# Residual rows added by the matrix unit inside the state-space stage, and a last stage that is one memory-to-memory copy

## The chip, the cores and the metric

One core of one Trainium2 chip. The metric is the device time of one launch in microseconds (us): 2570.66 us before, the median of 3 runs (2567.91 to 2570.71).

## The reference, cut to what matters

Two layers over 4096 rows (4 sequences of 1024) of 256 columns, float32. The second one is the place of the change:

```python
xn = _layernorm(x)
x = x + _L1_attn_ref(xn, ...) + _L1_ffn_ref(xn, ...)

def _L1_attn_ref(resid, ...):          # state-space layer
    xn = resid * rsqrt(mean(resid * resid) + eps) * norm_w
    skip = xn @ skip_w.T               # 256 -> 512
    x = xn @ in_w.T
    ...                                # causal convolution, silu, delta, B, C, scan over time
    y = (ys + W_D * x) * silu(skip)
    return resid + y @ out_w.T         # 512 -> 256

def _L1_ffn_ref(x, ...):               # 8 experts, the best 2 for each row, weighted sum
    ...
```

So the output is `x + xn` (called x1p in the kernel), plus the state-space rows `y @ out_w.T`, plus the experts' rows.

## The kernel before

Four stages follow each other, each a block that all engines enter and leave together: `layer0`, `mamba`, `experts`, `combine`. Rows are worked on in 8 chunks of T = 512 (NCH = 8, SUB = 4 groups of 128 rows in a chunk).

**layer0** computes the first layer, x1p = x + xn and what the second layer needs, and stores x1p, xn1, the transposed normed rows xrT (512 KB for each chunk) and the router's logits in device memory (L253 stores x1p).

**mamba** (up to about 1822 us) is a software pipeline of 256 steps u = 32 q + n: q is the chunk, n = 0 to 31 a step in it (channel half n // 16, state n % 16). In each step

- ScalarE makes two decays (L1204, `m_da`), two steps ahead, each of 128x512,
- GpSimd multiplies the step's input (L1058, `bx`, 128x1024), three steps ahead, into one of 5 buffers,
- VectorE runs two scans (L1339, `m_hh`), then multiplies by C (L1347, `hc`),
- TensorE, once VectorE's `hc` of step u has come, broadcasts the C row of step u + 1 into the one PSUM bank `cb` (`spread`, L1408), adds `hc` of step u into `y` (L1434, two matmuls), and then does at most one further piece (`pieces`).

`hc` of step u + 1 waits for `cb` of step u + 1. The pieces are the projections of neighbouring chunks; all of them go through one PSUM bank, `rb`, in an order fixed by the list `ahead`: in chunk q, SK0 to SK3 of chunk q + 1 after steps 0, 2, 4, 6 and IN0 to IN3 of chunk q + 2 after steps 24, 26, 28, 30 (both read `xr`), O0 and O1 of chunk q - 1 after steps 8 and 10 (the output product, L1389), BD and DT of chunk q + 1 after steps 14 to 22. A piece waits until its predecessor has been drained from `rb`, which ScalarE does (`take_in`, `take_skip`, `take_out` ...). The last O0 and O1 follow when the 256 steps are over. GpSimd also adds the convolution taps, does the sums of delta, and sends routed rows away by indirect DMA (`spread_rows`, L1067).

All loads and stores go through SyncE's queue, in an order written out by hand. In chunk q it reads:

```python
load_b(8 * q + 2); load_b(8 * q + 3)     # B rows, 1 MB broadcast, each waits for GpSimd
load_rows(SUB * q + 2)                   # waits for an earlier indirect DMA
if q + 2 < NCH: load_xr(q + 2)           # L906, waits for SK3 of chunk q + 1
load_b(8 * q + 4)
if q > 0: store_rows(q - 1, 0); store_rows(q - 1, 1)   # L926, wait for ScalarE's copy of O0, O1
...
```

**experts** computes the experts and adds their rows into `mo` in device memory by indirect DMAs with addition.

**combine** loads x1p and `mo` in 8 chunks of 512 rows (L1797), adds them on VectorE (L1808) and stores the sum to `out` (L1800), all through SyncE's queue.

Of the kernel before, what the change touches and what calls it, by code (L numbers as in the profile page):

```python
# [6 lines left out]
P = 128  # L7
F32 = mybir.dt.float32
# [4 lines left out]
ALU = mybir.AluOpType  # L13
# [5 lines left out]
D = 256  # L19
KD = D // P  # L20
T = 512
NCH = NTOK // T
CPS = SEQ // T
SUB = T // P
# [32 lines left out]
NJ = NTOK // P  # L57
# [676 lines left out]
KE = E_IN // P  # L734
# [14 lines left out]
def mamba(nc, dram):  # L749
# [5 lines left out]
    HALF = KE // 2  # L755
# [23 lines left out]
    with ExitStack() as ctx:  # L779
        def sb(name, shape, dt=F32):  # L780
            return ctx.enter_context(nc.sbuf_tensor("m_" + name, shape, dt))

        def sem(name):
            return ctx.enter_context(nc.semaphore("m_" + name))
# [4 lines left out]
        rb = ctx.enter_context(nc.psum_tensor("m_rb", [P, T], F32))  # L789
# [3 lines left out]
        w_out = sb("w_out", [P, KE, D])  # L793
        vec = sb("vec", [P, NV1])
        A = sb("A", [P, KE * NST])
        ident = sb("ident", [P, P])
        sel = sb("sel", [3 * 2 * NST, NST], BF16)
        xr = sb("xr", [P, KD, T])
        xpad = sb("xpad", [P, KE, PAD + 2 * T])

        spare = sb("spare", [P, 4, KE, T])
        cv, ez, w, lw = spare[:, 1], spare[:, 1], spare[:, 2], spare[:, 3]
        y1 = [[spare[:, 0, 0:HALF], spare[:, 0, HALF:KE]], [sb("y1", [P, HALF, T])[:]] * 2]
# [17 lines left out]
        mo = sb("mo", [P, 2, D])  # L821
# [24 lines left out]
        ext = part([P, NJ, EXT])  # L846
        onesrow = ones[:, 0:NPICK]
        ps_before, ps_total = y[:, 0], y[:, 1]
        vec_in, w_si_in = sem("vec_in"), sem("w_si_in")
        lg_in, s_c0, s_d, s_ex, s_mm, s_out = sem("lg_in"), sem("c0"), sem("d"), sem("ex"), sem("mm"), sem("plan_out")  # L850

# [12 lines left out]
        block = ctx.enter_context(nc.Block())  # L864
# [22 lines left out]
        @block.sync  # L887
        def _(sp):
            sp.dma_start(lg, dram["logits"]).then_inc(lg_in, 16)
            sp.dma_start(vec[:], dram["vec1"]).then_inc(vec_in, 16)  # L890
            sp.dma_start(w_si[:], dram["w_si"]).then_inc(w_si_in, 16)
            sp.dma_start(xr[:], dram["xrT"][0:P]).then_inc(xr_in, 16)
            for tile, src in w_loads:
                sp.dma_start(tile, src).then_inc(w_in, 16)

            def load_rows(j):
                if j >= NJ:
                    return
                if j >= 2:
                    sp.wait_ge(picks_out[j % 2], 16 * TOPK * (j // 2))  # L900
                sp.dma_start(rows[:, j % 2, 0:D], dram["xn1"][j * P:(j + 1) * P, :]).then_inc(rows_in[j % 2], 16)
                sp.dma_start(rows[:, j % 2, D:REC], dram["ext"][:, j, :]).then_inc(rows_in[j % 2], 16)

            def load_xr(p):
                wait_filled(sp, "SK3", p - 1)
                sp.dma_start(xr[:], dram["xrT"][p * P:(p + 1) * P]).then_inc(xr_in, 16)  # L906

            def store_b(p):
                sp.wait_ge(s_row, p + 1)
                sp.dma_start(bT[p], brow[0:NST]).then_inc(b_out, 16)  # L910

            def load_b(G):
                p, j = G // 8, G % 4
                if p >= NCH:
                    return
                if G % 8 == 0:
                    sp.wait_ge(b_out, 16 * (p + 1))
                if G >= 2:
                    sp.wait_ge(s_bx, (G - 1) * NG)
                src = bT[p:p + 1, j * NG:(j + 1) * NG, :].to_broadcast([P, NG, T])  # L920
                sp.dma_start(bb[:, G % 2], src).then_inc(b_in[G % 2], 16)

            def store_rows(p, j):
                wait_drained(sp, f"O{j}", p)
                at = T + p * T + 2 * j * P
                sp.dma_start(dram["mo"][at:at + 2 * P, :].rearrange("(s p) d -> p s d", p=P), mo[:]).then_inc(mo_out, 16)  # L926

            load_xr(1)
            store_b(0)
            sp.wait_ge(s_d, D_STEPS)  # L930
            sp.dma_start(dram["ext"], ext).then_inc(s_out, 16)
            sp.dma_start(dram["tex"], tex).then_inc(s_out, 16)
            sp.wait_ge(s_out, 32)
            load_rows(0)
            load_rows(1)
            load_b(0)
            load_b(1)
            for q in range(NCH):
                load_b(8 * q + 2)
                load_b(8 * q + 3)  # L940
                load_rows(SUB * q + 2)
                if q + 2 < NCH:
                    load_xr(q + 2)
                load_b(8 * q + 4)
                if q > 0:
                    store_rows(q - 1, 0)
                    store_rows(q - 1, 1)
                load_b(8 * q + 5)
                load_rows(SUB * q + 3)
                if q + 1 < NCH:  # L950
                    store_b(q + 1)
                load_b(8 * q + 6)
                load_b(8 * q + 7)
                load_rows(SUB * q + 4)
                load_b(8 * q + 8)
                load_b(8 * q + 9)
                load_rows(SUB * q + 5)
            store_rows(NCH - 1, 0)
            store_rows(NCH - 1, 1)
            sp.wait_ge(mo_out, 32 * NCH)  # L960
# [395 lines left out]
        def _(pe):  # L1356
            mm = pe.matmul
# [6 lines left out]
            def piece(g, p):  # L1364
                if turn[g, p] > 0:
                    pe.wait_ge(drained, turn[g, p])
                if g[:2] in ("IN", "SK"):
                    e = int(g[2:])
                    if g == "IN0":
                        pe.wait_ge(xr_in, p * 16 + 16)  # L1370
                    col = (E_IN if g[:2] == "IN" else 0) + e * P
                    for k in range(KD):
                        last = mm(rb[:], w_si[:, k, col:col + P], xr[:, k], start=(k == 0), stop=(k == KD - 1))
                elif g == "BD":
                    if p == 0:
                        pe.wait_ge(w_in, 16 * len(w_loads))
                    pe.wait_ge(s_silu, 2 * p + 1)
                    for e in range(KE):
                        last = mm(rb[0:DR + 2 * NST, :], w_x[:, e], xs[p % 2][:, e], start=(e == 0), stop=(e == KE - 1))
                elif g[:2] == "DT":  # L1380
                    e = int(g[2:])
                    wait_drained(pe, "BD", p)
                    last = mm(rb[:], w_dt[:, e * P:(e + 1) * P], dr, start=True, stop=True)
                else:
                    j = int(g[1:])
                    pe.wait_ge(s_y1, 2 * p + 2)
                    for s in (2 * j, 2 * j + 1):
                        for e in range(KE):
                            last = mm(rb[:, (s % 2) * D:(s % 2 + 1) * D], y1[e // HALF][p % 2][:, e % HALF, s * P:(s + 1) * P], w_out[:, e],  # L1389
                                      start=(e == 0 and s % 2 == 0), stop=(e == KE - 1 and s % 2 == 1), skip_group_check=True)  # L1390
                last.then_inc(filled, 1)

            def pieces(q, n):
# [26 lines left out]
            for u in range(STEPS):  # L1420
                q, n = u // NU, u % NU
# [4 lines left out]
                if n % NST == 0:  # L1426
# [3 lines left out]
                    for i in range(HALF):  # L1430
                        e = HALF * j + i
# [346 lines left out]
def combine(nc, dram, out):  # L1778

    with ExitStack() as ctx:  # L1780
        def sb(name, shape, dt=F32):
            return ctx.enter_context(nc.sbuf_tensor("c_" + name, shape, dt))

        def sem(name):
            return ctx.enter_context(nc.semaphore("c_" + name))

        xa = sb("xa", [P, NJ, D])
        mo = sb("mo", [P, NJ, D])
        x_in = [sem(f"x_in{i}") for i in range(NCH)]
        s_add, out_done = sem("add"), sem("out_done")  # L1790
        block = ctx.enter_context(nc.Block())

        @block.sync
        def _(sp):
            for c in range(NCH):
                for tile, src in ((xa, dram["x1p"]), (mo, dram["mo"][T:, :])):
                    sp.dma_start(tile[:, c * SUB:(c + 1) * SUB], src[c * T:(c + 1) * T, :].rearrange("(s p) d -> p s d", p=P)).then_inc(x_in[c], 16)  # L1797
            for c in range(NCH):
                sp.wait_ge(s_add, c + 1)
                sp.dma_start(out[c * T:(c + 1) * T, :].rearrange("(s p) d -> p s d", p=P), xa[:, c * SUB:(c + 1) * SUB]).then_inc(out_done, 16)  # L1800
            sp.wait_ge(out_done, 16 * NCH)

        @block.vector
        def _(dve):
            for c in range(NCH):
                cs = slice(c * SUB, (c + 1) * SUB)
                dve.wait_ge(x_in[c], 32)
                dve.tensor_tensor(xa[:, cs], xa[:, cs], mo[:, cs], ALU.add).then_inc(s_add, 1)  # L1808

# [67 lines left out]
```

## Time and profile before

| | us |
|---|---|
| median of 3 runs | 2570.66 (2567.91 to 2570.71) |
| profiled execution, its own time | 2571.51 |
| its span in the trace | 2569.8 |
| mean granted TensorE clock | 0.95 of full speed |
| TensorE matmul busy | 2128.3 (83%) |
| VectorE busy | 1967.2 (77%) |
| ScalarE busy | 1371.7 (53%) |
| GpSimd busy | 1330.0 (52%) |
| DMA moved | 290.84 MB, mean 113 GB/s |

### The profile page before, as it was taken

What the parts mean: (1) busy time and instruction counts of PE and PEld (TensorE: products, weight loads), DVE (VectorE), ACT (ScalarE), POOL (GpSimd) and SP (SyncE); (2) the same over time, 40 slices, a digit from 0 to 9 for tenths busy, and PEclk for the clock granted to TensorE, in tenths of its full rate; (3) what the DMA queues carried; (4) which work ended last, traced back from release to release, by engine and by line L of the source; (5) the groups of instructions that cost most, each with busy time, mean ns of one, the idle gap of its engine ahead of it and who ended that gap; (6) DMA issues with size and microseconds to landing.
All of it is one profiled execution on the core that took longest, in us unless ns stands there. A gap on an engine that the chain in (4) does not pass through costs nothing. (4 is left out here: it accounts for less than half of the span.)

```text
span 2569.8 us, 34895 instructions
## 1 busy us (share of the span) xinstructions
PE 2128.3 (83%) x10642; PEld 1527.3 (59%) x10642; DVE 1967.2 (77%) x2692; ACT 1371.7 (53%) x2333; POOL 1330.0 (52%) x953
## 2 busy tenths in 40 slices
PE   2699999999976788788888888766599999999991
PEld 1578777787742233333333333332499999999991
DVE  6654566444536999989999999999498888888882
ACT  1322233322346766666666666743377777677760
POOL 1102222022224999999999999996024333433331
PEclk8899999999987999999999999999799999999996
DMA  8010011100121213131313131321466666666746
GB/s 263 17 42 16 25 41 41 41 25 16 41 74 59 103 62 113 66 109 74 113 60 116 61 112 62 105 82 66 173 226 220 208 230 233 217 210 227 236 138 206
DMA packets 117336, 290.84 MB, mean 113 GB/s; under 512 B 20788, under 2 KB 93892, under 8 KB 98452
## 3 DMA queue, kind: packets, MB, share of 16 engines
q1 hardware_dynamic: 102964, 271.31, 30.0%
q0 software_dynamic: 14304, 18.75, 3.6%
q8 instruction: 26, 0.43, 0.1%
q14 instruction: 42, 0.34, 0.0%
HBM read 239.21 MB, written 50.82 MB: 113 GB/s over the span
## 5 line engine op out<-in xcount | busy, mean ns | idle before, releaser
L1058 POOL TENSOR_TENSOR m_work<-m_ux,m_bb 128x1024 f32<-128x1024 f32 x256 | 601.7, 2370 | 37.3 <-DVE m_ux L1317 18.8
L1434 PE MATMUL m_y<-m_work,m_ident 128*128 128x512 f32 x1024 | 498.2, 609 | 1.5 <-DVE m_work L1347 1.5
L1204 ACT ACTIVATE m_da<-m_dl,m_A 128x512 f32<-128x512 f32 x512 | 347.9, 685 | 278.3 <-DVE m_hh L1339 277.5
L1748 PE MATMUL e_h<-e_xTh,e_w1h 128*128 128x256 f32 x1248 | 353.3, 283 | 17.1 <-DVE e_xTl L1684 17.1
L1748 PE MATMUL e_h<-e_xTl,e_w1h 128*128 128x256 f32 x1248 | 349.4, 280 | 0.0
L1748 PE MATMUL e_h<-e_xTh,e_w1l 128*128 128x256 f32 x1248 | 349.2, 280 | 0.0
L1347 DVE TENSOR_TENSOR m_work<-m_hh,m_cb 128x1024 f32<-128x1024 f32 x256 | 312.7, 1222 | 37.7 <-PE m_cb L1408 13.7
L1339 DVE TENSOR_TENSOR_SCAN m_hh<-m_da,m_carry,m_work 128x512 f32<-128x512 f32 x256 | 313.8, 1267 | 11.5 <-POOL m_work L1058 11.5
L1339 DVE TENSOR_TENSOR_SCAN m_hh<-m_da,m_work 128x512 f32<-128x512 f32 x256 | 298.4, 1207 | 14.7 <-POOL m_work L1058 14.5
L1434 PEld LDWEIGHTS m_y<-m_work,m_ident 128*128 128x128 f32 x1024 | 198.8, 194 | 161.8 <-issue 149.8
L281 POOL TENSOR_TENSOR small<-mv,eps_ln 128x4 f32<-128x4 f32 x17 | 3.4, 199 | 551.8 <-DVE mv L399 551.8
L1408 PE MATMUL m_cb<-m_bc,m_sel 96*128 96x512 bf16 x256 | 98.2, 384 | 197.5 <-DVE m_work L1347 197.1
L1748 PEld LDWEIGHTS e_h<-e_xTh,e_w1h 128*128 128x128 f32 x1248 | 237.4, 190 | 17.7 <-DVE e_xTl L1684 17.3
L1647 ACT ACTIVATE e_sg<-e_h,e_b 128x256 f32<-128x256 f32 x312 | 145.8, 467 | 188.5 <-PE e_h L1748 188.5
L1677 DVE TENSOR_TENSOR e_w1l<-e_w,e_w1h 128x1024 fp32r<-128x1024 f32 x156 | 190.8, 1223 | 69.6 <-ACT e_w1h L1628 69.6
L1408 PEld LDWEIGHTS m_cb<-m_bc,m_sel 96*128 96x128 bf16 x256 | 24.7, 97 | 363.6 <-DVE m_work L1347 349.0
L1748 PEld LDWEIGHTS e_h<-e_xTl,e_w1h 128*128 128x128 f32 x1248 | 235.6, 189 | 0.0
L1748 PEld LDWEIGHTS e_h<-e_xTh,e_w1l 128*128 128x128 f32 x1248 | 235.4, 189 | 0.0
L1701 DVE SCALAR_TENSOR_TENSOR e_ac<-e_h,e_b,e_sg 128x256 f32<-128x256 f32 x312 | 149.2, 479 | 44.8 <-ACT e_sg L1647 44.2
L1759 PE MATMUL e_o<-e_w2h,e_ach 128*128 128x256 f32 x624 | 174.1, 279 | 0.0
L1534 POOL DMA_INDIRECT scratch_mo<-e_yo,e_place x78 | 160.8, 2061 | 24.4 <-issue 11.9
L1759 PE MATMUL e_o<-e_w2h,e_acl 128*128 128x256 f32 x624 | 173.3, 278 | 0.0
(263 smaller groups left out, 4755.9 us busy)
## 6 DMA issues: line engine op xcount, KB each, us to landing
e_w<-in_w SPq DMA_DIRECT2D x39, 2048.0 KB, 7.5
m_bb<-scratch_bT SPq DMA_DIRECT2D x64, 1024.0 KB, 4.6
e_w<-in_w SPq DMA_DIRECT2D x39, 1024.0 KB, 10.0
scratch_rec<-x1p SPq DMA_DIRECT2D x39, 260.0 KB, 8.1
e_xg<-scratch_rec SPq DMA_DIRECT2D x39, 260.0 KB, 2.7
e_b<-in_b SPq DMA_DIRECT2D x39, 128.0 KB, 3.0
xt<-in_x SPq DMA_DIRECT2D x9, 512.0 KB, 5.4
xres<-in_x SPq DMA_DIRECT2D x8, 512.0 KB, 4.8
```

Source lines behind the costliest of these rows:

```text
L1058: pool.tensor_tensor(bx[:, u % NB], ux[q % 2][:, cols], slot.to_broadcast([P, HALF, T]), ALU.mult).then_inc(s_bx, 1)
L1204: act.activation(da[d % NA][:], dl[q % 2][:, e], ACT.Exp, scale=A[:, at:at + 1]).then_inc(s_exp, 1)
L1339: dve.tensor_tensor_scan(hh[:, u % 2, i], da[d % NA][:], bx[:, u % NB, i], 0.0 if q % 2 == 0 else carry[:, n % NST, e:e + 1], ALU.mult, AL ...
L1347: dve.tensor_tensor(hc[:, u % 4], hh[:, u % 2], cb[:].rearrange("p (o t) -> p o t", o=1).to_broadcast([P, HALF, T]), ALU.mult).then_inc(s_ ...
L1408: mm(cb[:], sel[:, at:at + 1].to_broadcast([3 * 2 * NST, P]), bc3[q % 2][:], start=True, stop=True).then_inc(s_cb, 1)
L1434: last = mm(y[:, i], ident[:], hc[:, u % 4, i], start=False, stop=(n % NST == NST - 1))
L1534: pool.indirect_dma_start(dram["mo"][:, :], bass.IndirectOffsetOnAxis(ap=place[i][:, s:s + 1], axis=0), yo[i][:, s, :], None, compute_op=A ...
L1647: act.activation(sg[:, m % 2], hbank[m % HR][:, 1], ACT.Silu, bias=b1[i][:, KF + m:KF + m + 1]).then_inc(s_sg, 1)
L1677: dve.tensor_tensor(piece(w1l[i], mm), piece(w1[i], mm), f32(piece(w1h[i], mm)), ALU.subtract).then_inc(s_wl, 1)
L1701: dve.scalar_tensor_tensor(out=ac[:, m % 2], in0=hbank[m % HR][:, 0], scalar=b1[i][:, m:m + 1], in1=sg[:, m % 2], op0=ALU.add, op1=ALU.mul ...
L1748: last = mm(hbank[m % HR][:, j], w[i][:, k, cols], x[i][:, k], start=(p == 0 and k == 0 and j == 0), stop=(p == 2 and k == KD - 1 and j == 1),
L1759: last = mm(obank[i][:, s], a[i][:, m, s * P:(s + 1) * P], w[i][:, m], start=(m + s + p == 0), stop=(p == 2 and m == KF - 1 and s == NS - ...
```

## The change

In mamba, the residual rows x1p of chunk p are loaded into the place of `xr` (`xres` is the same memory, seen as 4 groups of 128 rows by 256 columns), and each O piece begins with two more matmuls, identity times residual rows, that open the accumulation in `rb`. So `mo` holds residual plus state-space rows before the experts add to it. As `xr` and `xres` share their memory, SyncE's order is changed: the residual's load stands where `load_xr` stood, and `load_xr` now follows the stores of O0 and O1. In combine, VectorE's additions and the SBUF tiles go; one DMA copies `mo` to `out`.

```diff
+        xres = xr[:].rearrange("p k t -> p (k t)").rearrange("p (s d) -> p s d", d=D)
...
+            def load_res(p):
+
+                if p + 2 < NCH:
+                    wait_filled(sp, "SK3", p + 2)
+                if p > 0:
+                    wait_filled(sp, "O1", p - 1)
+                sp.dma_start(xres, dram["x1p"][p * T:(p + 1) * T, :].rearrange("(s p) d -> p s d", p=P)).then_inc(res_in, 16)
...
                 load_rows(SUB * q + 2)
-                if q + 2 < NCH:
-                    load_xr(q + 2)
+                if q > 0:
+                    load_res(q - 1)
                 load_b(8 * q + 4)
                 if q > 0:
                     store_rows(q - 1, 0)
                     store_rows(q - 1, 1)
+                if q + 2 < NCH:
+                    if q > 0:
+                        wait_filled(sp, "O1", q - 1)
+                    load_xr(q + 2)
...
+            load_res(NCH - 1)
             store_rows(NCH - 1, 0)
             store_rows(NCH - 1, 1)
...
                     pe.wait_ge(s_y1, 2 * p + 2)
+                    pe.wait_ge(res_in, 16 * (p + 1))
                     for s in (2 * j, 2 * j + 1):
+                        at = slice((s % 2) * D, (s % 2 + 1) * D)
+                        mm(rb[:, at], ident[:], xres[:, s], start=(s % 2 == 0), stop=False, skip_group_check=True)
                         for e in range(KE):
-                            last = mm(rb[:, (s % 2) * D:(s % 2 + 1) * D], y1[e // HALF][p % 2][:, e % HALF, s * P:(s + 1) * P], w_out[:, e],
-                                      start=(e == 0 and s % 2 == 0), stop=(e == KE - 1 and s % 2 == 1), skip_group_check=True)
+                            last = mm(rb[:, at], y1[e // HALF][p % 2][:, e % HALF, s * P:(s + 1) * P], w_out[:, e],
+                                      start=False, stop=(e == KE - 1 and s % 2 == 1), skip_group_check=True)
...
 def combine(nc, dram, out):
...
-            for c in range(NCH):
-                for tile, src in ((xa, dram["x1p"]), (mo, dram["mo"][T:, :])):
-                    sp.dma_start(tile[:, c * SUB:(c + 1) * SUB], src[c * T:(c + 1) * T, :].rearrange("(s p) d -> p s d", p=P)).then_inc(x_in[c], 16)
-            for c in range(NCH):
-                sp.wait_ge(s_add, c + 1)
-                sp.dma_start(out[c * T:(c + 1) * T, :].rearrange("(s p) d -> p s d", p=P), xa[:, c * SUB:(c + 1) * SUB]).then_inc(out_done, 16)
-            sp.wait_ge(out_done, 16 * NCH)
+            sp.dma_start(out.rearrange("(p n) d -> p (n d)", p=P),
+                         dram["mo"][T:, :].rearrange("(p n) d -> p (n d)", p=P)).then_inc(out_done, 16)
+            sp.wait_ge(out_done, 16)
...
-                dve.tensor_tensor(xa[:, cs], xa[:, cs], mo[:, cs], ALU.add).then_inc(s_add, 1)
```

## Rows read from the trace of the kernel before

**Rows 1.** The page's 40 slices: busy tenths, granted clock, DMA.

```profile
DVE  6654566444536999989999999999498888888882
...
POOL 1102222022224999999999999996024333433331
PEclk8899999999987999999999999999799999999996
```

**Rows 2.** Issues of SyncE's queue: start us, us, engine line op out<-in.

```profile
1226.66 0.43 SPq L902 DMA_DIRECT2D m_rows<-scratch_ext  x1
1227.14 0.43 SPq L906 DMA_DIRECT2D m_xr<-scratch_xrT  x1
```

**Rows 3.** Timeline of TensorE around O0 and O1, chunk q = 3.

```profile
1225.26 1.88 PE L1434 MATMUL m_y<-m_work,m_ident 128*128 128x512 f32 x4
1226.97 1.03 PE L1389 MATMUL m_rb<-m_w_out,m_spare 128*128 128x256 f32 x4
1227.84 1.03 PE L1389 MATMUL m_rb<-m_w_out,m_y 128*128 128x256 f32 x4
...
1230.43 0.38 PE L1408 MATMUL m_cb<-m_bc,m_sel 96*128 96x512 bf16 x1
...
1237.79 0.38 PE L1408 MATMUL m_cb<-m_bc,m_sel 96*128 96x512 bf16 x1
```

**Rows 4.** Timeline of VectorE in the same steps; idle time and releaser in brackets.

```profile
1231.04 1.22 DVE L1347 TENSOR_TENSOR m_work<-m_hh,m_cb 128x1024 f32<-128x1024 f32 x1
1232.97 2.46 DVE L1339 TENSOR_TENSOR_SCAN m_hh<-m_da,m_carry,m_work 128x512 f32<-128x512 f32 x2 [0.71 <-POOL m_work L1058]
...
1239.20 1.22 DVE L1347 TENSOR_TENSOR m_work<-m_hh,m_cb 128x1024 f32<-128x1024 f32 x1
```

**Rows 5.** VectorE's waits after step 10 of chunk q = 2.

```profile
1107.60 2.34 DVE L1339 TENSOR_TENSOR_SCAN m_hh<-m_da,m_work 128x512 f32<-128x512 f32 x2 [0.97 <-POOL m_work L1058]
...
1119.44 2.34 DVE L1339 TENSOR_TENSOR_SCAN m_hh<-m_da,m_work 128x512 f32<-128x512 f32 x2 [0.73 <-POOL m_work L1058]
```

**Rows 6.** Time to landing of `load_xr` (L906), and of layer0's loads of 1 KB rows.

```profile
DMA to landing us min/median/max: 3.2/3.4/3.9
...
DMA to landing us min/median/max: 3.4/4.8/6.0
```

**Rows 7.** TensorE's matmuls behind idle times of 3.00 and 3.75 us.

```profile
1216.78 0.58 PE L1408 MATMUL m_cb<-m_bc,m_sel 96*128 96x512 bf16 x1 [3.00 <-DVE m_work L1347]
1217.16 3.14 PE L1434 MATMUL m_y<-m_work,m_ident 128*128 128x512 f32 x4
1220.13 1.88 PE L1373 MATMUL m_rb<-m_xr,m_w_si 128*128 128x512 f32 x4
...
1091.29 0.58 PE L1408 MATMUL m_cb<-m_bc,m_sel 96*128 96x512 bf16 x1 [3.75 <-DVE m_work L1347]
1091.67 3.62 PE L1434 MATMUL m_y<-m_work,m_ident 128*128 128x512 f32 x4
1095.09 2.74 PE L1373 MATMUL m_rb<-m_xr,m_w_si 128*128 128x512 f32 x4
```

**Rows 8.** Stretches: PE, PEld, DVE, ACT, POOL busy us, granted clock, DMA share, GB/s.

```profile
1091.00:1095.00 4.00, 3.71 (x5) 1.65 (x6) 3.61 (x4) 3.58 (x8) 3.92 (x3) 0.50 0.57 231
```

**Rows 9.** Waits of GpSimd in chunk q = 3 (1187.5 to 1313): total, times, longest.

```profile
POOL m_spare L1038 <- ACT m_spare L1182: 2.5, 1, 2.5
POOL m_spare L1032 <- ACT m_spare L1192: 2.1, 1, 2.1
```

**Rows 10.** The end of mamba, on TensorE.

```profile
1812.44 1.10 PE L1389 MATMUL m_rb<-m_w_out,m_spare 128*128 128x256 f32 x4 [1.41 <-DVE m_y L1325]
```

**Rows 11.** Stretches of combine, columns as in the eighth group.

```profile
2539.00:2542.00 3.00, 0.00 (x0) 0.00 (x0) 1.20 (x1) 0.00 (x0) 0.00 (x0) 0.50 1.10 349
...
2563.00:2566.00 3.00, 0.00 (x0) 0.00 (x0) 0.00 (x0) 0.00 (x0) 0.00 (x0) 0.50 1.09 385
```

**Rows 12.** All transfers of combine, window 2531 to 2570.

```profile
DMA packets 12672, 12.58 MB, mean 323 GB/s; under 512 B 384, under 2 KB 12672, under 8 KB 12672
```

More of the change, by code:

```diff
@@ L848, in mamba @@
         ps_before, ps_total = y[:, 0], y[:, 1]
+        res_in = sem("res_in")
         vec_in, w_si_in = sem("vec_in"), sem("w_si_in")
@@ L1780, in combine @@
     with ExitStack() as ctx:
[L1781 to L1790, printed above, removed]
+        out_done = ctx.enter_context(nc.semaphore("c_out_done"))
         block = ctx.enter_context(nc.Block())
@@ L1794, in _ @@
         def _(sp):
-            for c in range(NCH):
-                for tile, src in ((xa, dram["x1p"]), (mo, dram["mo"][T:, :])):
-                    sp.dma_start(tile[:, c * SUB:(c + 1) * SUB], src[c * T:(c + 1) * T, :].rearrange("(s p) d -> p s d", p=P)).then_inc(x_in[c], 16)
-            for c in range(NCH):
-                sp.wait_ge(s_add, c + 1)
-                sp.dma_start(out[c * T:(c + 1) * T, :].rearrange("(s p) d -> p s d", p=P), xa[:, c * SUB:(c + 1) * SUB]).then_inc(out_done, 16)
-            sp.wait_ge(out_done, 16 * NCH)
[L1803 to L1807, printed above, removed]
-                dve.tensor_tensor(xa[:, cs], xa[:, cs], mo[:, cs], ALU.add).then_inc(s_add, 1)
+            sp.dma_start(out.rearrange("(p n) d -> p (n d)", p=P),
+                         dram["mo"][T:, :].rearrange("(p n) d -> p (n d)", p=P)).then_inc(out_done, 16)
+            sp.wait_ge(out_done, 16)
 def kernel(**inputs):
```

## The prediction

> **What bounds the kernel now.** I read the page's slices first [rows 1]. In the state-space stage VectorE and GpSimd are both at 9 tenths and the granted clock is close to full; so what matters there is what delays VectorE. Combine, the last stage, has little VectorE work and much DMA work. The stage before it, the experts, is not touched. Two places therefore decide: combine, which is a plain transfer, and the steps around O0 and O1, where the change puts a wait and matmuls into TensorE's stream.
>
> Next the timelines of one chunk, q = 3, on three engines. TensorE starts O0 at 1226.97, straight behind the sum of step 8, and has the C row for step 10 in `cb` at 1230.43 + 0.38 = 1230.81 [rows 3]. VectorE starts `hc` of step 10 at 1231.04 [rows 4]. So TensorE is only 0.23 us ahead of VectorE there: whatever delays O0 by more delays VectorE. SyncE issues `load_xr` in that chunk at 1227.14, right behind the rows, whose issue hangs on an indirect DMA of GpSimd [rows 2]. That is the place that the residual's load gets. The load is thus issued in the very microsecond in which TensorE wants to begin O0. I looked at the other five chunks in which SyncE's queue stands so (q = 1, 2, 4, 5, 6): the two times are within 0.9 us of each other in all.
>
> Then what VectorE can get back. It waits for GpSimd 0.71 us after step 10 in this chunk [rows 4], 0.97 and 0.73 us in chunk 2 [rows 5]. GpSimd itself works without idle time from late in one chunk far into the next, then waits 2.1 and 2.5 us for ScalarE [rows 9], which follows VectorE's pace. A chunk's chain so runs over GpSimd in its first part and over VectorE in its second.
>
> **The change part by part.**
>
> *The wait for the residual, six chunks (q = 1 to 6).* `load_res` is issued when `load_xr` was, at 1227.14; its own wait, for SK3, was there before, and O1 of the chunk before is long over. Landing takes 3.2 to 3.9 us for `load_xr`, of the same 512 KB; layer0's loads with rows of 1 KB, as this one has, took 3.4 to 6.0, median 4.8, beside other traffic [rows 6]. I take 3.5, near the one in the same place. So TensorE, ready at 1226.97, begins at 1227.14 + 3.5 = 1230.6: 3.6 us late (bounds 3.4 and 5.0).
>
> *The clock.* TensorE now idles 3.6 us there. The nearest rows are idle times of 3.00 and 3.75 us [rows 7]. Behind the first, `cb` took 0.58 for 0.38 and the four records of `y` 3.14 for 1.88: 1.5 us more. Behind the second, 0.2 + 1.74 and then 2.74 for 1.88: 2.8 us more, and the granted clock was 0.50, the 1.2 GHz level, in the stretch behind it [rows 8]. For 3.6 us I take 2.3 (bounds 0 and 3).
>
> *The matmuls.* Two more a piece are four records of 128x256; four of these take 0.87 us from start to start [rows 3]. That is 0.87 for O0.
>
> Together O0 ends 3.6 + 2.3 + 0.9 = 6.8 us later. Less the 0.23 that TensorE was ahead, VectorE's `hc` of step 10 starts 6.5 us later. ScalarE's copy of O0, its store, and O1 follow. SyncE's `load_b` behind the load does not come later, as it waits for GpSimd anyway. Given back: VectorE's next waits for GpSimd, which works on during the stall, 0.7 or 0.97 + 0.73, mean 1.2. Lost again: O1 is 0.9 longer. `cb` of step 12 was done at 1238.17 [rows 3] and VectorE needed it at 1239.20, or 1238.5 without its 0.71 wait [rows 4]; so 0.6 is missing. A chunk costs 6.5 - 1.2 + 0.6 = 5.9 us, six cost 35.
>
> *Chunk q = 7.* Its load has no SK3 to wait for other than past ones, and the queue issues it early, so only the matmuls count: about 0.9 - 0.23 at O0 and the same at O1, 1.3 us.
>
> *The end of mamba.* O0 and O1 of the last chunk stand alone behind VectorE's last product [rows 10], with nothing beside them. The load of their residual lies many steps ahead. 2 x 0.87 = 1.7 us.
>
> *`load_xr` later.* It moves behind the stores of O0 and O1, to about step 12; IN0, which reads it, comes after step 24, over ten steps of about 3.7 us. The load is covered, and would cost its 3.4 us if it were not. `load_b` behind it was issued later than those stores before too. The 4 MB more of DMA traffic find the queue far from full. All this is 0.
>
> *combine.* The stage went from 2531.0 to the span's end, 38.8 us, for 12.58 MB [rows 12] at 349 GB/s while loads and stores mixed, 385 for stores alone [rows 11]. That is 8.39 / 349 + 4.19 / 385 = 34.9, as the first stores overlap the last loads about 36; some 2.8 us are start and end. VectorE's additions, 1.2 us each, lay beside the loads. The copy moves 4.19 MB. No row shows a copy from memory to memory. If an engine moves it as fast as a load or a store, it takes 4.19 / 385 = 10.9 us; if reading and writing share the rate, 8.39 / 385 = 21.8; one after the other, 12.0 + 10.9 = 22.9. The memory's side of the traffic, 8.39 MB, is to be moved either way, so I take 21.8. With 2.4 for start and end the stage is 24.2 us, 14.6 less than before (bounds 25.5 and 13.5).
>
> The Trainium skill, "DMA: Bandwidth & Descriptors", section "Latency and other measured facts", gives 207 to 214 GB/s per direction for copies between two HBM tensors at well-placed pitches. By that the copy would be an estimated 4.19 MB / 214 GB/s = 19.6 us instead of 21.8; no row here shows it.
>
> *Sum.* +35 +1.3 +1.7 -14.6 = +23.4 us, against the span of 2569.8. What lies around the span (2571.5 - 2569.8 = 1.7 us) stays. The profiled execution is 0.9 us above the median of the runs; against the median of 2570.7 the time is 2594.
>
> **The rivals.**
>
> *A, the forecast: 2594 us, chance 0.48.* Its own range is 2584 to 2604: 1.5 us either way in the six stalls.
>
> *B, the clock holds.* TensorE's idle time of 3.6 us brings no slower clock. The stall falls by 2.3 us in six chunks, 14 in all: 2580. For it: the two rows do not show what decides. Against it: the shorter idle time of 3.00 us already had slow matmuls behind it [rows 7]. Chance 0.12.
>
> *C, the copy runs at the full rate.* Then combine takes 10.9 + 2.4 us and gives 25.5: 2583. For it: each byte passes an engine once. Against it: the rates of 349 and 385 hardly depend on the direction, which looks like a limit that both sides share. Chance 0.20.
>
> *D, the load lands late.* At the 5.0 us bound, with 3 us of slow clock behind, a chunk costs 5.9 + 1.4 + 0.7 = 8.0: six 48, time 2607. For it: rows of 1 KB were slower in layer0 [rows 6]. Against it: the queue is nearly empty in this place. Chance 0.10.
>
> *E, faster: GpSimd's chain swallows the stall.* The one mechanism: GpSimd has no idle time through most of a chunk, and if it alone set the chunk's length, VectorE would lose at step 10 only what it would otherwise lose to GpSimd later. It decides from a giveback of 3.5 us per chunk on, where six chunks cost 5.9 + 1.2 - 3.5 = 3.6 each, 22, still above 14.6; a gain needs 5.2 us of giveback, cost 1.9 each, 11.5 with 3.0 for the rest: 2570.6. At a full 6.5 us of giveback, 0.6 each is left: 2562. Against it: VectorE's waits behind step 10 sum to no more than 0.7 to 1.7 us [rows 4, 5], and GpSimd waits for ScalarE later in the chunk [rows 9]. Chance 0.05.
>
> *F, the copy does not do what it says.* If the one DMA ran on a few engines only, or slower than the lowest bound, combine would lose instead: at a quarter of 385 it takes 43.6 + 2.4 us, 7 more than before, time 2616. Chance 0.05.
>
> **How the numbers follow.** The likeliest is A. B and C together with a mild stall end at 2569; D and F end at 2607 and 2616. The range that leaves out no more than 2 in 10 is 2572 to 2608. A measurement of this kernel can tell about 0.2%, 5 us, from no change; so slower means above 2576. A, D and F are slower, and B and C each alone. Both together, with short stalls, come close to no change. Faster 0.06 (E, and B with C at their low ends), same 0.07, slower 0.87.
>
> **What the changed profile would show.** The wait: TensorE idle about 3.6 us before the first record of O0 in six chunks, released by the DMA into `xr`'s place, none in q = 7. The clock: O0's records longer than 0.38 us each, granted clock 0.50 behind the idle time. The stall: VectorE's `hc` of step 10 idle some 6.5 us, released by `cb`, and no wait for GpSimd at step 11. The period of chunks q = 1 to 6 grows by 5.9 us. combine: one DMA, some 24 us from its issue to the end, VectorE idle. The prediction is wrong if the load of the residual is issued well ahead of O0, because GpSimd's indirect DMA comes earlier relative to TensorE than it does now; if the stall is given back by a chain that I did not see; or if the copy's rate is off the bounds.

## The result, and the profile after

The change makes the kernel slower: 2583.0 us (median of 5 runs) against 2570.7 us (median of 5), ratio 1.0046 with a 95% interval of 1.0035 to 1.0057. The profiled execution has a span of 2582.6 us.

The three stages that matter can be cut at fixed events: the first scan of mamba, the first instruction of the experts (`e_ident`), and the first issue of the last stage. The same three events stand in each of the tables below.

| span in us | before | after | difference |
|---|---|---|---|
| start to first scan (layer0, entry of mamba) | 818.3 | 822.9 | +4.6 |
| mamba, first scan to `e_ident` | 1005.4 | 1037.7 | +32.3 |
| experts | 707.3 | 706.8 | -0.5 |
| combine, first issue to the span's end | 38.8 | 15.2 | -23.6 |
| sum | 2569.8 | 2582.6 | +12.8 |

The first line is not touched by the change and is no effect of it: in the other kernels with the same mamba (e2, e7, e8) the first scan starts at 819.3, 818.0 and 817.8.

Chunk q = 3 after the change, first SyncE's queue (start us, us, engine line op out<-in), in the place of [rows 2]; this issue follows 0.1 us behind that of the rows (1241.87 + 0.43):

```profile
1242.40 0.38 SPq L916 DMA_DIRECT2D m_xr<-scratch_x1p  x1
```

TensorE around O0, for [rows 3]:

```profile
1240.55 1.88 PE L1452 MATMUL m_y<-m_work,m_ident 128*128 128x512 f32 x4
1246.64 0.67 PE L1405 MATMUL m_rb<-m_xr,m_ident 128*128 128x256 f32 x2 [4.21 <-DMA m_xr<-scratch_x1p]
...
1248.35 1.91 PE L1407 MATMUL m_rb<-m_w_out,m_y 128*128 128x256 f32 x4
...
1252.72 0.38 PE L1426 MATMUL m_cb<-m_bc,m_sel 96*128 96x512 bf16 x1
```

And VectorE at step 10, for [rows 4]; at step 12 it waits 0.92 us more:

```profile
1253.14 1.22 DVE L1362 TENSOR_TENSOR m_work<-m_hh,m_cb 128x1024 f32<-128x1024 f32 x1 [6.90 <-PE m_cb L1426]
```

Read them together. The load is issued while TensorE still works on step 8. TensorE then stands idle for 4.21 us, until the DMA lands. Its next records run slowly: four of them take 1.91 us where they took 1.03. VectorE, which at step 10 had waited for nothing, waits 6.90 us for the C row that TensorE writes only after O0. The same picture comes six times, once in each of q = 1 to 6, with VectorE's wait at 6.22, 8.12, 6.90, 7.13, 6.52 and 6.71 us. In q = 7, where the load was issued early enough, it is missing, and VectorE waits 1.10 us at step 10.

The granted clock behind the idle time, in the columns of [rows 8]:

```profile
1247.00:1251.00 4.00, 4.00 (x13) 3.21 (x12) 0.00 (x0) 1.32 (x2) 4.00 (x3) 0.58 0.47 193
```

All waits of VectorE in mamba (waiter, releaser, us in total, times, longest), after:

```profile
DVE m_work L1362 <- PE m_cb L1426: 58.4, 19, 8.1
DVE m_hh L1354 <- POOL m_work L1073: 14.5, 14, 2.1
```

The same view of the kernel before:

```profile
DVE m_hh L1339 <- POOL m_work L1058: 26.0, 27, 2.2
DVE m_work L1347 <- PE m_cb L1408: 13.7, 9, 2.6
```

So the waits for TensorE grew by 44.7 us and those for GpSimd shrank by 11.5; the difference, 33.2, is the 32.3 us that mamba lost, within 1 us. The six long waits are 41.6 of the 58.4.

The last stage has one DMA, issued at 2567.36. Its time to landing:

```profile
DMA to landing us min/median/max: 14.8/14.8/14.8
```

### The profile page after: what moved, and what is told of

It reads as the page before. It is cut to its first block and busy times, and to the rows that moved or that the text cites. A ratio compares the mean times of both kernels' runs of the same rounds, so it can differ in the third digit from the quotient of the medians.

```text
span 2582.6 us, 35010 instructions
## 1 busy us (share of the span) xinstructions
PE 2149.8 (83%) x10706; PEld 1545.7 (60%) x10706; DVE 1956.8 (76%) x2684; ACT 1376.8 (53%) x2333; POOL 1330.6 (52%) x953
## 5 line engine op out<-in xcount | busy, mean ns | idle before, releaser
L1073 POOL TENSOR_TENSOR m_work<-m_ux,m_bb 128x1024 f32<-128x1024 f32 x256 | 602.5, 2370 | 52.6 <-DVE m_hh L1354 31.3
L1452 PE MATMUL m_y<-m_work,m_ident 128*128 128x512 f32 x1024 | 492.1, 603 | 1.5 <-DVE m_work L1362 1.5
L1362 DVE TENSOR_TENSOR m_work<-m_hh,m_cb 128x1024 f32<-128x1024 f32 x256 | 312.8, 1222 | 81.5 <-PE m_cb L1426 58.4
## 6 DMA issues: line engine op xcount, KB each, us to landing
e_w<-in_w SPq DMA_DIRECT2D x39, 1024.0 KB, 10.1
```

The lines of the kernel that those rows point to most:

```text
L1073: pool.tensor_tensor(bx[:, u % NB], ux[q % 2][:, cols], slot.to_broadcast([P, HALF, T]), ALU.mult).then_inc(s_bx, 1)
L1362: dve.tensor_tensor(hc[:, u % 4], hh[:, u % 2], cb[:].rearrange("p (o t) -> p o t", o=1).to_broadcast([P, HALF, T]), ALU.mult).then_inc(s_ ...
L1452: last = mm(y[:, i], ident[:], hc[:, u % 4, i], start=False, stop=(n % NST == NST - 1))
```

## The experiments

All ratios are against the kernel before on the same chip. The runs were spread over several chips, on which the median of the kernel before was 2570.7 (beside the changed kernel), 2571.7 (beside e1 to e4), 2572.3 (e5 to e8) and 2574.0 us (e9, e10); so differences of 1 to 3 us between medians of different groups say nothing. Where mamba's length is given, it is from the first scan to `e_ident`, 1005.4 before and 1037.7 after.

**Each part alone.** e1 is the kernel before with the new combine, so its output lacks the residual. e2 is the changed mamba with the old combine, so the residual is added twice.

```diff
# e1: before, and in combine
-            (loads of x1p and mo in 8 chunks, additions, 8 stores)
+            sp.dma_start(out.rearrange("(p n) d -> p (n d)", p=P),
+                         dram["mo"][T:, :].rearrange("(p n) d -> p (n d)", p=P)).then_inc(out_done, 16)
```

> The kernel before with the new combine alone: one copy of mo to out; the output lacks the residual rows. Theory: the copy moves 4.19 MB at the rate at which loads and stores went before (349 GB/s), so combine takes 15.2 us as in the changed kernel and not 38.8: 23.6 us less than before, 2547 us. Rival: a part of the gain behind mamba in the changed kernel comes from elsewhere (experts' part, entry of the stage), and the copy alone gives the forecast 14.6: 2556 us.

Measured: 2550.2 us, ratio 0.9914 (0.9901 to 0.9927). Mamba 1005.6, the copy landed 15.0 us after its issue. In the trace the stage went from 38.8 to 15.4 us. The copy alone is worth 21.5 us in the medians, and clearly not 14.6.

> The changed mamba with the combine stage of before; the residual is added twice. Theory: mamba costs 36.8 us (33.3 in six stalls, 3.5 at the end), nothing of which is given back later: 2607 us. Rival: the stages are not independent, and the sum of both parts misses the 12.4 us of the whole change by more than 3 us.

Measured: 2603.7 us, ratio 1.0119 (1.0105 to 1.0134), 32.0 us above before; mamba 1038.1. The expectation of 2607 was 3 to 4 us too high, as it had put the 4.6 us of the untouched first stage into mamba. The parts add up: 32.0 - 21.5 = 10.5 us, against 12.4 measured for both. So the two parts are independent within 2 us.

**What the six stalls are made of.** Three kernels take it apart.

e5 has the load and the wait, but not the identity matmuls; the output lacks the residual.

```diff
                     pe.wait_ge(res_in, 16 * (p + 1))
-                        mm(rb[:, at], ident[:], xres[:, s], start=(s % 2 == 0), stop=False, skip_group_check=True)
...
-                                      start=False, stop=(e == KE - 1 and s % 2 == 1), skip_group_check=True)
+                                      start=(e == 0 and s % 2 == 0), stop=(e == KE - 1 and s % 2 == 1), skip_group_check=True)
```

> The changed kernel without the two identity matmuls of each O piece; the load and TensorE's wait for it stay; the output lacks the residual. Theory: wait and slow clock make 4.1 of the 5.5 us of a chunk, the matmuls 1.4 with O1's part, and the 3 us of the last chunk and the end go with them: 2571 us. Rival: the wait is what is given back by GpSimd's chain and the matmuls are the cost: 2555 us.

Measured: 2570.5 us, ratio 0.9992 (0.9982 to 1.0001). Mamba 1024.9, 12.8 us less than with the matmuls. So 19.5 of the 32.3 us are the wait and what it does to the clock, 12.8 the matmuls. VectorE's six waits at step 10 were still 5.38 to 7.29 us.

e6 fills the wait with four matmuls whose result is overwritten.

```diff
+                    if j == 0 and 0 <= p < NCH - 2:
+                        for i in range(4):
+                            mm(rb[:], ident[:], w_out[:, 0:2].rearrange("p k d -> p (k d)"), start=True, stop=True)
                     pe.wait_ge(res_in, 16 * (p + 1))
```

> The changed kernel with four matmuls of 128x512 (identity times output weights, overwritten afterwards) in front of the wait for the residual before O0 of the six chunks. They take 3.4 us, most of the wait. Theory: the granted clock stays up and O0 takes 4.3 us instead of 6.0 to 7.3, so a chunk is 2 us shorter: 2571 us. Rival: O0 is slow for another reason than the idle time (the first use of the loaded tile, the DMA traffic): O0 stays at 6 us and more, 2583 us or more.

Measured: 2572.8 us, ratio 1.0008 (0.9998 to 1.0017); mamba 1027.8, 9.9 us less than the changed kernel, with eight more records per chunk. TensorE in chunk 3:

```profile
1235.48 3.60 PE L1404 MATMUL m_rb<-m_w_out,m_ident 128*128 128x512 f32 x8
1239.57 0.70 PE L1408 MATMUL m_rb<-m_xr,m_ident 128*128 128x256 f32 x2 [0.49 <-DMA m_xr<-scratch_x1p]
...
1243.99 0.38 PE L1429 MATMUL m_cb<-m_bc,m_sel 96*128 96x512 bf16 x1
```

O0 now takes 1243.99 - 1239.57 = 4.42 us, as in all six chunks of this kernel; in the changed kernel it took 5.96, 7.34, 6.08, 6.02, 6.08 and 5.88, mean 6.23. The load still stands at the same place in the queue, and TensorE still waits 0.33 to 1.24 us for it behind the four matmuls. So the slow O0 came from the long idle time in front of it, and not from the freshly loaded tile: 1.8 us a chunk, 11 us in six, of which mamba shows 9.9.

An idle time of this length doesn't always bring the slow clock. The same mamba ran in three more traces (e2, e7, e8). Of the 24 O0s behind the wait, 22 took 5.8 to 7.4 us. Two took 4.39, in chunk 3 of e2 and of e7, behind idle times of 3.77 and 3.78 us; in e2 the granted clock was 1.00 from 1243 to 1251:

```profile
1243.25 0.67 PE L1405 MATMUL m_rb<-m_xr,m_ident 128*128 128x256 f32 x2 [3.77 <-DMA m_xr<-scratch_x1p]
...
1247.64 0.38 PE L1426 MATMUL m_cb<-m_bc,m_sel 96*128 96x512 bf16 x1
```

e10 doubles the matmuls, in the kernel e4 below, where no wait is left; it counts the residual twice.

```diff
+                        mm(rb[:, at], ident[:], xres[:, s], start=False, stop=False, skip_group_check=True)
                         last = mm(rb[:, at], ident[:], xres[:, s], start=False, stop=(s % 2 == 1), skip_group_check=True)
```

> The kernel with both moves, with every identity matmul done twice, so that the residual is counted twice in the output. It prices the matmuls alone. Theory: TensorE has no slack left at steps 10 and 12, so each piece's two more matmuls, 0.86 us, go fully into VectorE's wait for the C row: 1.7 us in each of seven chunks and at the end, 14 us more than 2547, 2561 us. Rival: TensorE still has slack or GpSimd's chain gives it back: 5 us more or less, 2552 us.

Measured: 2560.0 us, ratio 0.9950 (0.9936 to 0.9963), 13.1 us above e4's 2547.0; mamba 1016.5, 14.6 more. The matmuls cost what their records say, once TensorE's slack is used up:

```profile
1235.41 1.22 DVE L1362 TENSOR_TENSOR m_work<-m_hh,m_cb 128x1024 f32<-128x1024 f32 x1 [1.63 <-PE m_cb L1429]
```

This wait at step 10 of chunk 3 was 0.77 in e4, and the next, at step 12, 1.78 here and 0.79 there: 0.86 and 0.99 more for 0.86 us of matmuls each.

**Whether the wait can be avoided.** e3 moves the identity matmuls, and the wait with them, to the end of the piece; the loads stay.

```diff
-                    pe.wait_ge(res_in, 16 * (p + 1))
                     for s in (2 * j, 2 * j + 1):
                         at = slice((s % 2) * D, (s % 2 + 1) * D)
-                        mm(rb[:, at], ident[:], xres[:, s], start=(s % 2 == 0), stop=False, skip_group_check=True)
                         for e in range(KE):
...
+                    pe.wait_ge(res_in, 16 * (p + 1))
+                    for s in (2 * j, 2 * j + 1):
+                        at = slice((s % 2) * D, (s % 2 + 1) * D)
+                        last = mm(rb[:, at], ident[:], xres[:, s], start=False, stop=(s % 2 == 1), skip_group_check=True)
```

> The changed kernel with the two identity matmuls of each O piece at its end, and the wait for the residual only in front of them; loads as they are. Theory: what costs is that TensorE stands idle before O0; the eight output matmuls now take 3.5 us of the 3.9 to 4.2 us wait, the clock stays up, and a chunk costs 1 us instead of 5.5: mamba +9 over before, 2556 us in all. Rival: the matmuls themselves or GpSimd's chain make the 5.5 us: 2575 us or more.

Measured: 2552.6 us, ratio 0.9926 (0.9913 to 0.9939); mamba 1007.4, only 2.0 above before where 9 were expected. The output matmuls cover the load but for 0.25 to 0.64 us in four chunks and nothing in two.

e4 does this and issues the load before `load_rows`; e9 makes only the second move, with the identity matmuls first as in the changed kernel.

```diff
# e9: the changed kernel, and in SyncE's queue
-                load_rows(SUB * q + 2)
                 if q > 0:
                     load_res(q - 1)
+                load_rows(SUB * q + 2)
```

> The same as the one with the identity matmuls last, and the residual's load is issued ahead of load_rows, so that it hangs on SK3 alone and not on GpSimd's indirect DMA. Theory: it lands some 3 us earlier, no wait is left, only the matmuls cost: 0.5 us a chunk, mamba +6, 2553 us. Rival: the rows' load behind the wait for SK3 comes later and GpSimd's spreading of rows waits for it: no better than the other, 2556 us or more.

> The changed kernel with one line moved: the residual's load is issued ahead of load_rows; the identity matmuls stay first in each O piece. Theory: the load's place behind GpSimd's indirect DMA is the cause; issued on SK3 alone it lands 0 to 1 us before TensorE wants O0 (it was issued 4.7 us before O0 in chunk 3 of the kernel with the matmuls last), so nothing waits and the time is that of the kernel with both moves: 2547 to 2550 us. Rival: the residual lands too late for a first place in the piece by a us or two in most chunks, with some slow clock: 2555 us or more.

Measured: e4 2547.0 us, ratio 0.9899 (0.9885 to 0.9914), mamba 1001.9, which is 3.5 below before where 6 above were expected (the giveback, below, says why); e9 2548.9 us, ratio 0.9904 (0.9888 to 0.9919), mamba 1004.1. The two can't be told apart, nor from e1 without any residual (2550.2). (The execution of e9 that was profiled took 2555.0, since its experts took 714.1 us and not 707; its mamba is not concerned.) SyncE's queue of e9 in chunk 3, then TensorE:

```profile
1223.17 0.38 SPq L916 DMA_DIRECT2D m_xr<-scratch_x1p  x1
1227.40 0.33 SPq L903 DMA_DIRECT2D m_rows<-scratch_xn  x1
```

```profile
1227.84 0.59 PE L1405 MATMUL m_rb<-m_xr,m_ident 128*128 128x256 f32 x2
...
1232.16 0.38 PE L1426 MATMUL m_cb<-m_bc,m_sel 96*128 96x512 bf16 x1
```

Issued 4.7 us ahead of O0, the load leaves no idle time, and O0 takes its 4.3 us; so it is in chunks 1, 3 and 5. In chunks 2, 4 and 6 it is issued 4.3 to 4.5 us ahead and TensorE still waits 0.44 to 0.60 us, and VectorE 1.76 to 2.00 us at step 10 instead of 0.76 or 0.77. One line's place in the queue is worth 2583.0 - 2548.9 = 34 us in the medians, and 1037.7 - 1004.1 = 33.6 in mamba. e4 and e9 beat both kernels, by 1.0% the one before and by 1.3 to 1.5% the changed one.

A variant in which the residual has its own place in SBUF, 4 KB more per partition, was not tried.

**The copy.** e7 does the last copy twice, one after the other; e8 does it in rows of 1 KB.

```diff
# e7
             sp.wait_ge(out_done, 16)
+            (the same dma_start again)
+            sp.wait_ge(out_done, 32)
# e8
-            sp.dma_start(out.rearrange("(p n) d -> p (n d)", p=P),
-                         dram["mo"][T:, :].rearrange("(p n) d -> p (n d)", p=P)).then_inc(out_done, 16)
+            sp.dma_start(out.rearrange("(s p) d -> p s d", p=P),
+                         dram["mo"][T:, :].rearrange("(s p) d -> p s d", p=P)).then_inc(out_done, 16)
```

> The changed kernel with the last copy done twice, the second after the first has landed. Theory: a copy of 4.19 MB costs 12 us of transfer and 2.8 us until it has landed: 14.8 us more, 2598 us. Rival: a copy from memory to memory starts slowly or is paid for largely in fixed cost, and the second, warm one takes under 12 us.

> The changed kernel with the last copy in 4096 pieces of 1 KB rows instead of 64 KB pieces. Theory: the engines' rate by bytes is the limit and 1 KB is large enough, as it was for the loads and stores of the old combine at 349 to 385 GB/s: 0 to 1.5 us more than the changed kernel, 2583 to 2585 us. Rival: the high rate of the copy is owed to its large pieces, and with rows of 1 KB reading and writing share the rate: 10 us more, 2593 us.

Measured: e7 2596.5 us, ratio 1.0106 (1.0087 to 1.0125), 13.4 above the changed kernel's median (its four runs spread from 2594.1 to 2604.0, so the trace is the better measure); the two issues:

```profile
2562.34 0.61 SPq L1804 DMA_DIRECT2D out<-scratch_mo  x1
2577.33 0.51 SPq L1807 DMA_DIRECT2D out<-scratch_mo  x1
```

15.0 us apart, and the span ends 15.0 us after the second: a copy costs that, warm or not. e8 2581.4 us, ratio 1.0042 (1.0027 to 1.0056), the same as the changed kernel within the intervals; the copy in 1 KB rows landed after 15.3 us. Its many small packets show the traffic in time, 40 slices of the window 2562 to 2580:

```profile
GB/s 0 0 0 0 0 80 75 287 328 371 389 378 371 373 350 337 323 323 337 323 335 339 328 344 328 321 319 339 350 371 387 378 273 178 82 7 0 0 0 0
```

While it runs, the copy moves 319 to 389 GB/s, the same as loads and stores between memory and SBUF did [rows 11]. Neither the size of the pieces nor a shared rate of reading and writing plays a part.

## Why the prediction was right or wrong

**The direction and the reason were right.** Slower, by a wait for the residual in six chunks, at the place and for the cause named: the load is issued in the microsecond in which TensorE wants O0. e9 shows it: moving the issue alone takes the loss away.

**The wait of 3.6 us** was 3.65, 3.93, 4.21, 4.25, 3.83 and 3.98, mean 4.0. The step was sound; the landing in place took 3.9 to 4.2 us and not 3.5.

**The clock, 2.3 us of the stall,** was 6.23 - 4.42 = 1.8 on average, by e6. Rival B, that the clock holds, is out for the kernel as a whole; it is true of 2 O0s in 24.

**The matmuls, 0.87 us each piece,** hold by e10. O1's share at step 12 was put at 0.6 us and is 0.92 or 1.16 in each of the six chunks.

**Step 10 as a whole** was put at 6.5 us and measured 6.9.

**The giveback** was put at 1.2 us a chunk and was more than twice that. The prediction took VectorE's waits behind step 10 as 0.7 us in chunk 3 and 0.97 + 0.73 in chunk 2. Chunk 3 has 0.69 us more before its scans of step 14, at 1244.79; and four chunks have a third wait, for TensorE, at step 16. In chunk 2 before (TensorE, then VectorE):

```profile
1123.24 0.38 PE L1408 MATMUL m_cb<-m_bc,m_sel 96*128 96x512 bf16 x1 [2.28 <-DVE m_work L1347]
1123.45 2.96 PE L1434 MATMUL m_y<-m_work,m_ident 128*128 128x512 f32 x4
...
1130.72 1.22 DVE L1347 TENSOR_TENSOR m_work<-m_hh,m_cb 128x1024 f32<-128x1024 f32 x1 [1.67 <-PE m_cb L1408]
```

VectorE's wait for GpSimd at step 14 makes TensorE idle 2.28 us; the next records run slowly (granted clock 0.69, then 0.60), and the C row of step 16 comes 1.67 us late. The same place after the change:

```profile
1140.18 0.38 PE L1426 MATMUL m_cb<-m_bc,m_sel 96*128 96x512 bf16 x1 [1.46 <-DVE m_work L1362]
1140.39 1.88 PE L1452 MATMUL m_y<-m_work,m_ident 128*128 128x512 f32 x4
```

Before, chunks 1 to 6 lose 10.1 us to GpSimd at steps 11 and 14, and chunks 2, 4, 5 and 6 lose 1.58 to 1.67 us each, 6.5 in sum, to TensorE at step 16. e1, with the mamba of before, has all of these waits; the changed kernel has none of them, nor has any other kernel in which mamba was changed, but for one of 0.24 us in e4. That is 16.6 us, 2.8 a chunk. That the stall at step 10 lets GpSimd get ahead, and that this keeps TensorE's idle time short and its clock up, is read from the rows in their order; no run takes it apart further. It is the part of rival E that was true. Its full form, that GpSimd's chain sets the chunk's length, is out, as GpSimd's waits for VectorE's scans rose from 15.9 to 31.3 us instead.

**Mamba in sum** was put at +38 us and measured +32.3 in this trace, 32.7 in e2. From VectorE's first product of a chunk to that of the next, chunks 1 to 6 grew by 28.9 us, 4.8 each against a forecast of 5.9; chunk 7 by 1.8 against 1.3; the end by 1.8 against 1.7. So what mamba was over-priced by lies in the six chunks, and there in the giveback. The same giveback is the main reason that e4, with more matmuls than the kernel before, has a shorter mamba (1001.9 against 1005.4): its waits at steps 10 and 12 sum to 12.6 us, less than the 16.6 that are gone. A smaller part is uneven: at step 2 a slow clock of TensorE makes VectorE wait 1.3 to 1.6 us in some chunks (2.3 to 2.8 in chunk 0), and in how many differs between the kernels (at 1199.28 the kernel before has such a wait of 1.38 us, behind four records that took 3.35 us; e4 took 1.98 for them and has none). What decides it no run shows; these waits sum to 7.0 us before, 8.5 after and 5.5 in e4.

**The step that failed is the copy's term.** That the stage becomes one plain transfer was right, how fast it goes was not. The prediction took 21.8 us for the transfer, reading and writing sharing 385 GB/s, and 24.2 for the stage; the stage took 15.2, near rival C's 13.3. The argument for sharing, that the rates hardly depend on the direction, does not bear: e8 shows the copy at a load's rate while it reads and writes each byte. The start and end were too small as well. The old stage's transfers sum to 34.9 us, and the prediction raised that to 36 for an overlap that could only shorten it; 38.8 - 34.9 leaves 3.9 us for start and end, and 10.9 + 3.9 = 14.8 us is what the copy took to land. The estimate by the Trainium skill ("DMA: Bandwidth & Descriptors", "Latency and other measured facts"), 207 to 214 GB/s per direction for copies between HBM tensors, was off in the same way here, for one contiguous copy where the page's row is for tiles of 128 partitions: 4.19 MB in 14.8 us with start and end is 283 GB/s, and e8's slices stand at 319 and more while it runs.

Together: +23.4 forecast, +12.4 measured. Of the difference of 11.0 us, 9.0 are the copy and 5.7 mamba's sum; the first stage's 4.6 us and the spread between runs go the other way. The direction was no luck. That the size came out no further off was in part, as the first stage's 4.6 us are no effect of the change. Rival C had 2583 to the microsecond, and that was luck: its copy was nearly right, and its mamba, 5.7 us too dear, made up for the first stage's 4.6.

## What to carry to other kernels

When a buffer is shared to save memory, the load that fills it inherits the place of the one that it displaces; look in the trace at the microsecond in which its consumer is ready, and at whatever unrelated wait stands before it in the queue. Here moving one line let it go more than 4 us ahead of its consumer, and turned a loss of 12 us into a gain of 25 (e9 against the kernel before on its own chip, 2574.0 - 2548.9). A wait on the matrix unit is dearer than its length, since the work behind it mostly starts at the lower clock: 4.0 us of idle time cost 5.8. And a stall can pay part of itself back where another engine was behind: look past the stall for every wait that it may dissolve, those for the stalled engine too.

## What the runs showed of the hardware

A DMA from device memory to device memory moves 4.19 MB in 14.6 to 15.0 us with pieces of 64 KB (e1, e3 to e7, e9, e10 and the changed kernel) and in 15.3 us with rows of 1 KB, at 319 to 389 GB/s in the middle of it: the rate of one-way traffic, though the memory is both read and written. Through SBUF, with the addition, the same output cost 38.8 us.

Behind TensorE's idle times of 3.65 to 4.25 us the changed kernel's O0 took 5.9 to 7.3 us instead of 4.4 (records at half speed first, the 1.2 GHz level, and at full speed, the 2.4 GHz level, behind them; granted clock 0.58 from 1247 to 1251), six times of six; over the four traces with this mamba it was 22 of 24, and twice, behind 3.77 and 3.78 us, the clock stayed at the 2.4 GHz level. Shorter idle times had it too: behind 2.28 us at step 14 of the kernel before, the granted clock was 0.69 and then 0.60. Filling the idle time with four matmuls whose result nobody reads made the whole kernel 10 us faster than leaving it idle.
